# Two of K's three row blocks by seven block products instead of eight, with the sums on GpSimd

## The chip, the cores and the metric

The kernel runs on one core of one Trainium2 chip. The metric is the device time of one execution in microseconds (us); of several executions the median is taken.

## The reference

x is 64 batches of 32 rows by 512; ctx_4096 is 64 batches of 257 rows by 512. Six stages follow one another, each added to x. The change lies in the first, a cross attention in float32:

```
hidden = concat([context, latents])            # 257 + 32 = 289 rows per batch, 512 wide
q = latents @ Wq.T    -> 16 heads of 96        # latents = layernorm(x), 32 rows
k = hidden  @ Wk.T    ->  4 heads of 96        # 384 columns
v = hidden  @ Wv.T    ->  4 heads of 96
attn = softmax(q k^T / sqrt(96));  out = attn v @ Wo.T
```

After it come a self attention with rotary embedding, a linear layer with LoRA, a gated mix that uses a top-20 mask of ctx_4096 (the mask is computed during the first stage), a second self attention and a sparse linear layer.

## The kernel before

`phase_a` computes the cross attention for 16 tiles t of 128 rows, four batches j = 0 to 3 each; `phase_rest` does the other stages. Every engine's program is written out by hand as a list of stages, and semaphores join them: each engine runs its list strictly in order, so a stage that waits holds up everything behind it on its engine. `over_tiles` writes tile 0 and tile 15 out and loops over the others.

For one batch, TensorE (PE) forms K transposed (384 rows by 289 columns) as three row blocks of 128, each from four matmuls over the 512 contraction rows (`k_part`, L345), and V as two blocks (`v_part`, L352). K and V go through the two banks of `psKV` in turn: `next_bank` makes PE wait until the fill before last has been copied out. ScalarE (ACT) copies them out (`evac_k`, L505; `evac_v`, L513). `scores(t, j, h)` (L363) handles two of the four heads; VectorE (DVE) takes the row maxima (`row_max`, L637), ACT the exponentials (`exps`, L537), GpSimd (POOL) gathers the last 33 columns (`gather_tails`, L298), PE transposes the probabilities (`turn_probs`, L371 and L374), multiplies with V (`values`, L386 to L390), and turns a batch's output (`turn_out`, L411), which DVE copies to `OT` (`evac_ot`, L658). Once per tile PE runs the projection (`project`, L417) and the queries of the next tile (`q`, L335). DVE spends the rest of its time on the top-20 mask (`topk`, L678 and L682, eight steps per batch).

The K of batch j + 1 is made during batch j: row blocks 0 and 1 after `scores(t, j, 0)`, block 2 after `values(t, j, 0)`. The K of batch 0 is made at the head of the tile, where there are also the projection of the tile before and both V blocks. On ACT, the copy of block 2 stands behind `exps(t, j, 1)`. On DVE, batch j + 1 runs `evac_out`, `row_max(.., 0)`, top-k step 1, `evac_ot`, step 2, for j = 1 the row statistics of the next tile (`norm_stats`) and for j = 2 its normalisation (`norm`, L612), then `row_max(.., 1)` and steps 3 to 8. A float32 matmul shows as two passes in the trace, so one K block is 8 MATMUL rows.

```
def next_bank(t, n):
    wait(pe, kv_evac, kv(t, n) - 1)
    return psKV[:, kv_bank(t, n), :]
```

Of the kernel before, what the change touches and what calls it, by code (L numbers as in the profile page):

```python
# [10 lines left out]
ALU = mybir.AluOpType  # L11
# [20 lines left out]
GONE = -3.0e38  # L32

K_ROWS = [(0, 0, 96), (1, 64, 96), (1, 0, 64), (2, 0, 64), (3, 0, 96), (2, 64, 96)]
PARTS = [(0, 0, 0, 96, 0), (1, 0, 96, 128, 64), (1, 1, 0, 64, 0), (2, 1, 64, 128, 0), (3, 2, 0, 96, 0),
         (2, 2, 96, 128, 64)]
# [8 lines left out]
EARLY_LOADS, LATE_LOADS = 9, 11  # L47
# [10 lines left out]
def build_program(nc, a):  # L58
    ctx = ExitStack()
    with ctx:  # L60
# [19 lines left out]
        early_in = sem("early_in")  # L80
        n1 = norm_sems(sem, "n1")
# [6 lines left out]
        phase_a(nc, a, X, mask, ident, neghalf, x_tile, ps, early, early_in, n1, qkv_filled)  # L88
        phase_rest(nc, a, X, mask, ident, neghalf, x_tile, ps, early, early_in, n1, qkv_filled)


def phase_a(nc, a, X, mask, ident, neghalf, x_tile, ps, early, early_in, n1, qkv_filled):

    ctx = ExitStack()
    with ctx:
# [11 lines left out]
        hid = sb("hid", [P, TB, DC, S])  # L107
        xn = sb("xn", [P, D])
        xnT = sb("xnT", [P, DC, P])
        QT = sb("QT", [HD, KVH, TB, G * L])  # L110
        KT = sb("KT", [HD, 2, KVH, S])
        V = sb("V", [P, 2, 2, KW])
        Vlat = sb("Vlat", [P, KW])
# [52 lines left out]
        kv_evac = sem("kv_evac")  # L166
        s_filled = sem("s_filled")
# [18 lines left out]
        def kv(t, n):  # L186


            if isinstance(t, int) and t == 0 and n < 5:
                return 1 + n  # L190
            if isinstance(t, int) and t == -1 and n > 20:
                return 6 + n - 21
            return 4 + 24 * t + n
# [24 lines left out]
        def _(sp):  # L218
# [24 lines left out]
            def load_tail(t):  # L243
# [6 lines left out]
                wait(sp, kv_evac, kv(t - 1, 20) + 1)  # L250
# [8 lines left out]
            def body(t, first, last):  # L259
                if last:  # L260

                    for k, name in (("w_qkv", "w_qkv0"), ("w_o", "w_o0"), ("w_ffn", "w_ffn0"), ("loraA", "loraA"),
                                    ("cos", "cos"), ("sin", "sin"), ("causal", "causal"), ("block16", "block16"),
                                    ("jmask", "jmask")):
                        sp.dma_start(early[k][:], a[name]).then_inc(early_in, 16)
                    return
                for j in range(TB):
                    sp.wait_ge(kv_filled, kv(t, 5 * j + 4) + 1)
                    sp.wait_ge(topk_step, 8 * (TB * t + j) + 2)
                    sp.dma_start(hid[:, j, :, 0:CTX], a["ctxT"][TB * (t + 1) + j]).then_inc(ctx_in[j], 16)  # L270
# [5 lines left out]
        def _(pool):  # L276
# [4 lines left out]
            pool.wait_ge(zero_done, 4)  # L281

# [16 lines left out]

            def body(t, first, last):  # L300
                for j in range(TB):
                    for h in range(2):
                        if (j, h) == (1, 1):
                            next_rstd() if last else rstd_of(t + 1)
                        gather_tails(t, j, h)

            rstd_of(0)
            over_tiles(pool, body)

        @block.tensor  # L310
        def _(pe):
# [11 lines left out]
            def v_latents(t):  # L323
                out = next_bank(t - 1, 20)
# [5 lines left out]
            def q(t, k):  # L330
                out = next_bank(t - 1, 21 + k)
# [7 lines left out]
            def k_part(t, j, k):  # L339
                out = next_bank(t, 5 * j + k)  # L340
                if k == 0:
                    pe.wait_ge(ctx_in[j], 16 * (t + 1))
                    pe.wait_ge(m_evac, m_xt(t) + 1)
                for c in range(DC):
                    mm = pe.matmul(out[:, 0:S], WkT[:, c, P * k:P * k + P], hid[:, j, c, :],  # L345
                                   start=(c == 0), stop=(c == DC - 1))
                mm.then_inc(kv_filled, 1)

            def v_part(t, j, s):
                out = next_bank(t, 5 * j + 3 + s)  # L350
# [5 lines left out]
            def scores(t, j, h):  # L356
# [3 lines left out]
                if h == 0:  # L360
                    pe.wait_ge(kv_evac, kv(t, 5 * j + 2) + 1)
# [15 lines left out]
            def values(t, j, g):  # L377
                b = TB * t + j
                pe.wait_ge(pt_evac, 4 * b + g + 1)
                if g == 0:  # L380
                    pe.wait_ge(kv_evac, kv(t, 5 * j + 4) + 1)
# [17 lines left out]
            def next_qkv():  # L399
                pe.wait_ge(kv_evac, kv(NT - 1, 19) + 1)  # L400
# [30 lines left out]
            def body(t, first, last):  # L431
# [4 lines left out]
                k_part(t, 0, 2)  # L436
                v_part(t, 0, 0)
                v_part(t, 0, 1)
                if first:
# [3 lines left out]
                    pe.wait_ge(kv_evac, kv(-1, 23) + 1)  # L443
# [54 lines left out]
        def _(act):  # L498
            def evac_k(t, j, k):
                act.wait_ge(kv_filled, kv(t, 5 * j + k) + 1)  # L500
                if k == 0:
                    wait(act, s_filled, 2 * (TB * t + j) - 2)
                for g, tile, lo, hi, at in PARTS:
                    if tile == k:
                        ins = act.activation(KT[at:at + hi - lo, j % 2, g, :], psKV[lo:hi, kv_bank(t, 5 * j + k), 0:S],  # L505
                                             ACT.Copy)
                ins.then_inc(kv_evac, 1)

            def evac_v(t, j, s):
                act.wait_ge(kv_filled, kv(t, 5 * j + 3 + s) + 1)  # L510
                if s == 0:
                    wait(act, av_done, 4 * (TB * t + j) - 4)
                act.activation(V[:, j % 2, s, :], psKV[:, kv_bank(t, 5 * j + 3 + s), 0:KW], ACT.Copy).then_inc(kv_evac, 1)  # L513

            def evac_v_latents(t):
                wait(act, vtail_in, 16 * TAIL_LOADS * t)
                act.wait_ge(kv_filled, kv(t - 1, 20) + 1)
                act.activation(Vlat[:], psKV[:, kv_bank(t - 1, 20), 0:KW], ACT.Copy).then_inc(kv_evac, 1)

            def evac_q(t, k):  # L520
                wait(act, s_filled, 2 * TB * t)
                act.wait_ge(kv_filled, kv(t - 1, 21 + k) + 1)
# [1143 lines left out]
```

## Time and profile before

| what | before |
|---|---|
| three runs | 2140.99 us median (2138.29 to 2141.76) |
| profiled execution | 2136.47 us |
| its span, first to last instruction | 2134.4 us |
| granted TensorE clock, mean | 0.989 of full |
| PE, PEld (weight loads) busy | 96%, 69% of the span |
| DVE, ACT, POOL busy | 61%, 32%, 12% |
| K matmuls (L345) | 404.0 us busy, 1536 passes |
| POOL instructions | 360 |

The page gives busy time by engine, then groups of instructions by source line with their count, mean duration and the idle time of the engine ahead of them with the one that ended it. PE is busy nearly all the time up to about 1490 us, where `phase_a` ends. POOL's row of 40 slices reads 0 over that whole stretch. The timeline lists instructions in order of time; equal neighbours are merged, so the start of the next row less the start of a row is the pace at which the engine went through it, while the duration in the row also holds the drain of the last one.

### The profile page before, as it was taken

To read this page: it belongs to the slowest core of one execution; us is meant where nothing else is said; L and a number is where in the kernel's file an instruction comes from. 1 tells how busy PE (TensorE), PEld (TensorE's weight loads), DVE (VectorE), ACT (ScalarE), POOL (GpSimd) and SP (SyncE) were. 2 spreads that over 40 slices of the span, in tenths; PEclk is the share of its full clock that TensorE was granted. 3 is DMA by queue.
4 is the path that set the end of the run, shared out by engine and by line. 5 is a ranking of instruction groups with operands and counts; after the bars stand their busy time and mean duration, and the time that the engine had idled before them with its cause. 6 is when DMAs were issued, how large, how long until landed. Compare 5 with 4: busy or idle time off the path is not lost. (4 is left out here: it accounts for less than half of the span.)

```text
span 2134.4 us, 33623 instructions
## 1 busy us (share of the span) xinstructions
PE 2059.4 (96%) x10660; PEld 1480.4 (69%) x10660; DVE 1308.7 (61%) x4451; ACT 683.7 (32%) x1861; POOL 248.3 (12%) x360
## 2 busy tenths in 40 slices
PE   7999999999999999999999999999899999779998
PEld 5778677777767778677777867777566666466665
DVE  3736547484654747456483755747577777677885
ACT  2333333333332433333242433333223223122222
POOL 0000000000000000000000000000233333133332
PEclk9999999999999999999999999999999999889999
DMA  7101000010000101001010000120100000000000
GB/s 289 31 15 31 23 24 30 24 30 24 24 20 24 30 24 30 24 24 30 14 37 16 30 23 24 30 86 1 45 1 1 1 0 29 0 1 21 21 15 25
DMA packets 51991, 62.14 MB, mean 29 GB/s; under 512 B 14193, under 2 KB 47665, under 8 KB 51042
## 3 DMA queue, kind: packets, MB, share of 16 engines
q1 hardware_dynamic: 51938, 61.46, 9.1%
q8 instruction: 31, 0.51, 0.1%
q14 instruction: 22, 0.18, 0.0%
HBM read 54.00 MB, written 4.29 MB: 27 GB/s over the span
## 5 line engine op out<-in xcount | busy, mean ns | idle before, releaser
L345 PE MATMUL psLane<-hid,WkT 128*128 128x289 f32 x1536 | 404.0, 408 | 0.0
L352 PE MATMUL psLane<-WvT,hid 128*128 128x384 f32 x1024 | 348.7, 486 | 0.0
L345 PEld LDWEIGHTS psLane<-hid,WkT 128*128 128x128 f32 x1536 | 284.1, 190 | 72.7
L352 PEld LDWEIGHTS psLane<-WvT,hid 128*128 128x128 f32 x1024 | 189.8, 190 | 109.7
L537 ACT ACTIVATE probs<-psLane,nmax 128x289 f32<-128x289 f32 x256 | 126.2, 498 | 423.6 <-DVE nmax L640 423.6
L505 ACT ACTIVATE KT<-psLane 96x289 f32<-96x289 f32 (+2 forms) x384 | 155.8, 406 | 153.3 <-PE psLane L345 151.0
L298 POOL TENSOR_TENSOR tails<-probs,unit 128x66 f32<-128x66 f32 x128 | 38.1, 297 | 1387.3 <-ACT probs L537 1387.3
L678 DVE MAX8 top<-work 128x8 f32<-128x257 f32 x512 | 180.3, 414 | 2.7
L335 PE MATMUL psLane<-xnT,WqT 128*128 128x128 f32 x1536 | 176.6, 275 | 0.0
L335 PEld LDWEIGHTS psLane<-xnT,WqT 128*128 128x128 f32 x1536 | 174.8, 192 | 0.3
L663 DVE TENSOR_TENSOR X<-X,psLane 128x512 f32 (+1 forms) x16 | 11.0, 689 | 261.6 <-PE psLane L417 261.6
L417 PE MATMUL psLane<-WoT,OT 128*128 128x512 f32 x384 | 167.5, 592 | 1.4 <-DVE OT L658 1.4
L652 DVE TENSOR_TENSOR O<-psLane,rinv 128x384 f32<-128x384 f32 x64 | 35.7, 558 | 187.3 <-PE psLane L390 172.3
L363 PE MATMUL psLane<-KT,QT 96*128 96x289 f32 x512 | 146.1, 407 | 1.3 <-ACT QT L526 1.3
L513 ACT ACTIVATE V<-psLane 128x384 f32<-128x384 f32 x128 | 62.9, 491 | 243.2 <-PE psLane L352 243.2
L417 PEld LDWEIGHTS psLane<-WoT,OT 128*128 128x128 f32 x384 | 72.9, 190 | 89.8 <-issue 84.2
L637 DVE TENSOR_REDUCE rmax<-psLane 128x2 f32<-128x578 f32 x128 | 97.1, 758 | 58.7 <-PE psLane L363 57.5
L386 PEld LDWEIGHTS psLane<-V,probsT 128*128 128x128 f32 x512 | 87.3, 190 | 40.7 <-ACT probsT L544 8.5
L363 PEld LDWEIGHTS psLane<-KT,QT 96*128 96x128 f32 x512 | 90.8, 190 | 22.7 <-issue 7.2
L682 DVE MATCH_REPLACE8 work<-top,work 128x257 f32<-128x257 f32 x256 | 102.2, 411 | 0.0
L682 DVE MATCH_REPLACE8 work<-top,hid 128x257 f32<-128x257 f32 x256 | 102.2, 411 | 0.0
L682 DVE MATCH_REPLACE8 work<-top_last,work 128x257 f32<-128x257 f32 x256 | 102.2, 410 | 0.0
(190 smaller groups left out, 3138.2 us busy)
## 6 DMA issues: line engine op xcount, KB each, us to landing
hid<-in_ctxT SPq DMA_DIRECT2D x64, 514.0 KB, 3.8
y<-X SPq DMA_DIRECT2D x16, 256.0 KB, 2.0
X<-in_x SPq DMA_DIRECT2D x1, 3840.0 KB, 14.9
WqT<-in_WqT SPq DMA_DIRECT2D x4, 768.0 KB, 11.4
WoT<-in_WoT SPq DMA_DIRECT2D x1, 3072.0 KB, 21.7
Vtail<-Vlat SPq DMA_DIRECT2D x128, 24.0 KB
w_qkv<-in_w_qkv SPq DMA_DIRECT2D x2, 1536.0 KB, 6.5
w_ffn<-in_w_ffn SPq DMA_DIRECT2D x2, 1024.0 KB, 8.0
```

What stands on the lines that cost most here:

```text
L335: mm = pe.matmul(out[:, P * r:P * r + P], WqT[:, c, w:w + P], xnT[:, c, :], start=(c == 0), stop=(c == DC - 1))
L345: mm = pe.matmul(out[:, 0:S], WkT[:, c, P * k:P * k + P], hid[:, j, c, :], start=(c == 0), stop=(c == DC - 1))
L352: mm = pe.matmul(out[:, 0:KW], hid[:, j, c, P * s:P * s + P], WvT[:, c, :], start=(c == 0), stop=(c == DC - 1))
L363: mm = pe.matmul(psS[:, g % 2, 0:S], QT[:, g, j, :], KT[:, j % 2, g, :], start=True, stop=True)
L386: pe.matmul(out, probsT[:, g % 2, 0, :], V[:, j % 2, 0, cols], start=(g % 2 == 0), stop=False)
L417: mm = pe.matmul(psM, OT[:, n // G, n % G].rearrange("p j q -> p (j q)"), WoT[:, n, :], start=(n == 0), stop=(n == NKT * G - 1))
L505: ins = act.activation(KT[at:at + hi - lo, j % 2, g, :], psKV[lo:hi, kv_bank(t, 5 * j + k), 0:S], ACT.Copy)
L513: act.activation(V[:, j % 2, s, :], psKV[:, kv_bank(t, 5 * j + 3 + s), 0:KW], ACT.Copy).then_inc(kv_evac, 1)
L537: act.activation(probs[:, g, :], psS[:, g % 2, 0:S], ACT.Exp, bias=nmax[:, g:g + 1], scale=XSCALE, accum_out=rsum[:, j % 2, g:g + 1]).then ...
L637: dve.tensor_reduce(rmax[:, 2 * h:2 * h + 2], psS[:, :, 0:S], AX.X, ALU.max).then_inc(rmax_done, 1)
L678: ins = dve.max(top[step // 2][:, c, :], src[:, c, :] if step == 1 else work[:, c, :])
L682: ins = dve.match_replace(work[:, c, :], picked[:, c, :], src[:, c, :] if step == 2 else work[:, c, :], GONE)
```

## The change

Rows 0 to 255 of K (blocks m = 0, 1 of 128 rows), the contraction (k = 0, 1 of 256) and the 290 columns (s = 0, 1 of 145; one column of zeros is added) are cut in two each. The eight products of 2 by 2 block matrices are replaced by seven (Winograd's form of Strassen's scheme): four sums of weight blocks, made once (`combine_weights`), four sums of hidden blocks per batch (`sum_columns`), seven products, and seven sums of products (`add_products`). All sums run on POOL. The third row block is made as before. Per batch, PE now fills five banks for K: fill 0 is the third row block; fills 1, 2 and 3 hold products (1, 6), (7, 5) and (3, 4); fill 4 holds product 2. ACT copies fill 0 straight to `KT` in two instructions and each other fill to `kproducts` in one; POOL's last eight instructions per batch write the rest of `KT`, and `scores(t, j, 0)` waits for them. K's rows now stand in the order of the heads, so a head's 96 rows may lie at other partitions: `QT` and `KT` have 128 partitions, the foreign rows are set to zero once, and Q is copied out in seven pieces per tile, before six. The buffers of the sums lie in the space of `w_o` and `w_ffn` of the next stage, whose loads come later: SP waits for the last K before it issues them.

```
+KH = (S + 1) // 2
+K_FILLS = ((0,), (1, 6), (7, 5), (3, 4), (2,))
-EARLY_LOADS, LATE_LOADS = 9, 11
+EARLY_LOADS, LATE_LOADS = 7, 11
# SP, last tile
+                    sp.wait_ge(kv_filled, kv(NT - 1, 25) + 1)
+                    sp.wait_ge(k_ready, 8 * B)
+                    for k, name in (("w_o", "w_o0"), ("w_ffn", "w_ffn0")):
+                        sp.dma_start(early[k][:], a[name]).then_inc(square_in, 16)
# POOL
+            pool.memset(QT[:], 0.0).then_inc(rows_cleared, 1)
+            pool.memset(KT[:], 0.0).then_inc(rows_cleared, 1)
+            def sum_columns(t, j):
...
+                pool.wait_ge(ctx_in[j], 16 * (t + 1))
+                pool.wait_ge(m_evac, m_xt(t) + 1)
...
+                pool.tensor_tensor(ksums[:, 0], columns(0, 1), columns(0, 0), ALU.subtract).then_inc(ksum_step, 1)
+                pool.tensor_tensor(ksums[:, 2], columns(1, 1), columns(0, 1), ALU.subtract).then_inc(ksum_step, 1)
+                pool.wait_ge(ksum_step, 4 * b + 2)
+                pool.tensor_tensor(ksums[:, 1], columns(1, 1), ksums[:, 0], ALU.subtract).then_inc(ksum_step, 1)
+                pool.wait_ge(ksum_step, 4 * b + 3)
+                pool.tensor_tensor(ksums[:, 3], ksums[:, 1], columns(1, 0), ALU.subtract).then_inc(ksum_step, 1)
+            def k_block(t, j, m, s, x, y, op, done):
+                n = KH - s
+                for i, (g, tile, lo, hi) in enumerate(part for part in K_PARTS if part[1] == m):
+                    wait(pool, k_ready, 8 * (TB * t + j) + done + i)
+                    pool.tensor_tensor(KT[lo:hi, j % 2, g, KH * s:KH * s + n], x[lo:hi, 0:n], y[lo:hi, 0:n], op)\
+                        .then_inc(k_ready, 1)
+            def add_products(t, j):
+                b = TB * t + j
+                pool.wait_ge(kv_evac, kv(t, 7 * j + 1) + 1)
+                pool.tensor_tensor(u2, product(1), product(6), ALU.add).then_inc(kpost_step, 1)
+                pool.wait_ge(kv_evac, kv(t, 7 * j + 2) + 1)
+                pool.wait_ge(kpost_step, 3 * b + 1)
+                pool.tensor_tensor(u3, u2, product(7), ALU.add).then_inc(kpost_step, 1)
+                pool.wait_ge(kpost_step, 3 * b + 2)
+                pool.tensor_tensor(u4, u2, product(5), ALU.add).then_inc(kpost_step, 1)
+                pool.wait_ge(kpost_step, 3 * b + 3)
...
+                k_block(t, j, 1, 1, u3, product(5), ALU.add, 0)
+                pool.wait_ge(kv_evac, kv(t, 7 * j + 3) + 1)
+                k_block(t, j, 0, 1, u4, product(3), ALU.add, 2)
+                k_block(t, j, 1, 0, u3, product(4), ALU.subtract, 4)
+                pool.wait_ge(kv_evac, kv(t, 7 * j + 4) + 1)
+                k_block(t, j, 0, 0, product(1), product(2), ALU.add, 6)
+                pool.wait_ge(k_ready, 8 * b + 8)
             def body(t, first, last):
+                add_products(t, 0)
+                sum_columns(t, 1)
                 for j in range(TB):
+                    gather_tails(t, j, 0)
+                    if j == TB - 1 and not last:
+                        sum_columns(t + 1, 0)
+                    if j == 1:
+                        next_rstd() if last else rstd_of(t + 1)
+                    gather_tails(t, j, 1)
+                    if j < TB - 1:
+                        add_products(t, j + 1)
+                    if j < TB - 2:
+                        sum_columns(t, j + 2)
# PE
+                    for i, n in enumerate(K_FILLS[f]):
+                        if n == 6:
+                            pe.wait_ge(ksum_step, 4 * (TB * t + j) + 4)
...
+                        mm = k_product(out[:, KH * i:KH * i + KH], j, n)
                 if h == 0:
+                    pe.wait_ge(k_ready, 8 * b + 8)
                     if j < TB - 1:
                         k_part(t, j + 1, 0)
+                        k_part(t, j + 1, 1)
                         if j:
                             turn_out(t, j - 1)
-                        k_part(t, j + 1, 1)
...
                     if j < TB - 1:
                         k_part(t, j + 1, 2)
+                        k_part(t, j + 1, 3)
                         values(t, j, 1)
+                        k_part(t, j + 1, 4)
# ACT, behind exps(t, j, 1)
                         evac_k(t, j + 1, 2)
+                        evac_k(t, j + 1, 3)
+                        evac_k(t, j + 1, 4)
```

In the lists of instructions below, L-numbers are those of each kernel's own source, one row is one matmul (two passes of the trace) or one instruction of POOL, and the brackets name the semaphores waited for. `w_o` and `w_ffn` stand for the buffers of the sums: `w_o` holds the sums of hidden, `w_ffn` those of the weights and the products.

The program of tile 0 is shown. PE in batch j = 1, from the first K block behind `scores(t, 1, 0)` on, before:

```order
L345 MATMUL psLane<-hid,WkT 128x289 [waits m_evac,ctx_in2,kv_evac]
L345 MATMUL psLane<-hid,WkT 128x289 x3
L411 MATMUL psLane<-ident,O 128x128 [waits o_evac,m_evac]
L411 MATMUL psLane<-ident,O 128x128 x2
L345 MATMUL psLane<-hid,WkT 128x289 [waits kv_evac]
L345 MATMUL psLane<-hid,WkT 128x289 x3
L371 MATMUL psLane<-ident,probs 128x128 [waits pt_evac,exp_done]
L371 MATMUL psLane<-ident,probs 128x128
L371 MATMUL psLane<-ident,probs 128x128 [waits pt_evac,exp_done]
L371 MATMUL psLane<-ident,probs 128x128
L374 MATMUL psLane<-ident,tails 66x128 [waits tails_ready]
L363 MATMUL psLane<-KT,QT 128x289 [waits exp_done]
```

and now, from fill 1 on:

```order
L437 MATMUL psLane<-hid,WkT 128x145 [waits kv_evac]
L437 MATMUL psLane<-hid,WkT 128x145
L437 MATMUL psLane<-w_o,w_ffn 128x145 [waits ksum_step]
L437 MATMUL psLane<-w_o,w_ffn 128x145
L520 MATMUL psLane<-ident,O 128x128 [waits o_evac,m_evac]
L520 MATMUL psLane<-ident,O 128x128 x2
L480 MATMUL psLane<-ident,probs 128x128 [waits pt_evac,exp_done]
L480 MATMUL psLane<-ident,probs 128x128
L480 MATMUL psLane<-ident,probs 128x128 [waits pt_evac,exp_done]
L480 MATMUL psLane<-ident,probs 128x128
L483 MATMUL psLane<-ident,tails 66x128 [waits tails_ready]
L472 MATMUL psLane<-KT,QT 128x289 [waits exp_done]
```

The transposes of the output, L411 before and L520 now, stood between the two K blocks and now stand behind fill 1, whose second product waits for POOL's sums.

PE in the same batch from `values` on, before:

```order
L386 MATMUL psLane<-V,probsT 128x96 [waits vtail_in,o_evac,kv_evac,pt_evac]
L387 MATMUL psLane<-V,probsT 128x96
L345 MATMUL psLane<-hid,WkT 128x289 [waits kv_evac]
L345 MATMUL psLane<-hid,WkT 128x289 x3
L386 MATMUL psLane<-V,probsT 128x96 [waits pt_evac]
L387 MATMUL psLane<-V,probsT 128x96
L390 MATMUL psLane<-Vtail,probsTail 128x192
L352 MATMUL psLane<-WvT,hid 128x384 [waits kv_evac]
L352 MATMUL psLane<-WvT,hid 128x384 x3
```

and now:

```order
L437 MATMUL psLane<-w_o,w_ffn 128x145 [waits kv_evac]
L437 MATMUL psLane<-w_o,w_ffn 128x145 x3
L437 MATMUL psLane<-hid,w_ffn 128x145 [waits kv_evac]
L437 MATMUL psLane<-hid,w_ffn 128x145
L437 MATMUL psLane<-w_o,WkT 128x145 x2
L495 MATMUL psLane<-V,probsT 128x96 [waits pt_evac]
L496 MATMUL psLane<-V,probsT 128x96
L499 MATMUL psLane<-Vtail,probsTail 128x192
L437 MATMUL psLane<-hid,WkT 128x145 [waits kv_evac]
L437 MATMUL psLane<-hid,WkT 128x145
L460 MATMUL psLane<-WvT,hid 128x384 [waits kv_evac]
L460 MATMUL psLane<-WvT,hid 128x384 x3
```

Before, a V block stood behind `values(.., 1)`, and it took the bank of K's row block 1. Now fill 4 stands there (the last but one pair of rows), and takes the bank of fill 2, which was filled only just before.

POOL in tile 0, from its start to the end of its tails, before:

```order
L286 TENSOR_TENSOR rstd<-veps,neghalf 128x1 [waits veps_ready,zero_done]
L298 TENSOR_TENSOR tails<-probs,unit 128x66 [waits exp_done] x2
L298 TENSOR_TENSOR tails<-probs,unit 128x66 [waits pt_filled,exp_done]
L286 TENSOR_TENSOR rstd<-veps,neghalf 128x1 [waits veps_ready,xn_ready]
L298 TENSOR_TENSOR tails<-probs,unit 128x66 [waits pt_filled,exp_done] x5
```

and now, from the row statistics within batch 1 to the start of batch 2:

```order
L304 TENSOR_TENSOR rstd<-veps,neghalf 128x1 [waits veps_ready,xn_ready]
L316 TENSOR_TENSOR tails<-probs,unit 128x66 [waits pt_filled,exp_done]
L362 TENSOR_TENSOR w_ffn<-w_ffn 128x145 [waits kv_evac]
L365 TENSOR_TENSOR w_ffn<-w_ffn 128x145 [waits kpost_step,kv_evac]
L367 TENSOR_TENSOR w_ffn<-w_ffn 128x145 [waits kpost_step]
L355 TENSOR_TENSOR KT<-w_ffn 64x144 [waits k_ready,s_filled,kpost_step]
L355 TENSOR_TENSOR KT<-w_ffn 64x144 [waits k_ready]
L355 TENSOR_TENSOR KT<-w_ffn 128x144 [waits k_ready,kv_evac]
L355 TENSOR_TENSOR KT<-w_ffn 32x144 [waits k_ready]
L355 TENSOR_TENSOR KT<-w_ffn 64x145 [waits k_ready] x2
L355 TENSOR_TENSOR KT<-w_ffn 128x145 [waits k_ready,kv_evac]
L355 TENSOR_TENSOR KT<-w_ffn 32x145 [waits k_ready]
```

Behind the second gather of batch 1 there now stand the eleven instructions of `add_products(t, 2)`, each of which waits for the one before it.

## Rows read from the trace of the kernel before

**Rows 1.** The page, part 1: busy us (share of the span) x instructions.

```profile
PE 2059.4 (96%) x10660; PEld 1480.4 (69%) x10660; DVE 1308.7 (61%) x4451; ACT 683.7 (32%) x1861; POOL 248.3 (12%) x360
```

**Rows 2.** Waits of PE up to 1500 us: total us, times, longest.

```profile
PE psLane L386 <- DMA Vtail<-Vlat: 1.9, 1, 1.9
```

**Rows 3.** Groups: line, shape, count, busy us, mean ns, idle before; copies of K.

```profile
L505 ACT ACTIVATE KT<-psLane 96x289 f32<-96x289 f32 x128 | 51.8, 405 | 80.1 <-PE psLane L345 80.1
```

**Rows 4.** Timeline of PE, one tile: start us, us, engine, line, operation.

```profile
599.75 1.14 PE L363 MATMUL psLane<-KT,QT 96*128 96x289 f32 x4
...
657.91 3.74 PE L335 MATMUL psLane<-xnT,WqT 128*128 128x128 f32 x32
...
692.05 1.14 PE L363 MATMUL psLane<-KT,QT 96*128 96x289 f32 x4
```

**Rows 5.** Timeline of PE, batches 1 and 2 of that tile.

```profile
616.48 1.14 PE L363 MATMUL psLane<-KT,QT 96*128 96x289 f32 x4
617.46 2.12 PE L345 MATMUL psLane<-hid,WkT 128*128 128x289 f32 x8
619.42 0.49 PE L411 MATMUL psLane<-ident,O 128*128 128x128 f32 x3
...
621.70 0.60 PE L371 MATMUL psLane<-ident,probs 128*128 128x128 f32 x4
...
622.24 1.14 PE L363 MATMUL psLane<-KT,QT 96*128 96x289 f32 x4
...
623.71 2.14 PE L345 MATMUL psLane<-hid,WkT 128*128 128x289 f32 x8
...
626.46 2.75 PE L352 MATMUL psLane<-WvT,hid 128*128 128x384 f32 x8
...
633.39 1.14 PE L363 MATMUL psLane<-KT,QT 96*128 96x289 f32 x4
...
647.71 1.14 PE L363 MATMUL psLane<-KT,QT 96*128 96x289 f32 x4
```

**Rows 6.** Timeline of DVE, batch 1, and the normalisation in batch 2.

```profile
617.66 0.76 DVE L637 TENSOR_REDUCE rmax<-psLane 128x2 f32<-128x578 f32 x1 [0.36 <-PE psLane L363]
...
620.10 0.54 DVE L658 COPY OT<-psLane 128x384 f32<-128x384 f32 x1
...
622.15 0.68 DVE L601 BATCH_NORM_STATS2 stats<-X 128x6 f32 x1
...
623.42 0.76 DVE L637 TENSOR_REDUCE rmax<-psLane 128x2 f32<-128x578 f32 x1 [0.18 <-PE psLane L363]
...
639.05 0.54 DVE L612 TENSOR_SCALAR xn<-X,mv,rstd 128x512 f32 x1
```

**Rows 7.** Timeline of ACT and of POOL, batch 1: exponentials and tails.

```profile
624.42 0.50 ACT L537 ACTIVATE probs<-psLane,nmax 128x289 f32<-128x289 f32 x1 [0.86 <-DVE nmax L640]
...
625.57 0.30 POOL L298 TENSOR_TENSOR tails<-probs,unit 128x66 f32<-128x66 f32 x1 [1.71 <-ACT probs L537]
```

**Rows 8.** Groups of POOL: 66, 640, 512 columns, and the power of one.

```profile
L298 POOL TENSOR_TENSOR tails<-probs,unit 128x66 f32<-128x66 f32 x128 | 38.1, 297 | 1387.3 <-ACT probs L537 1387.3
...
L981 POOL TENSOR_TENSOR lanes<-lanes 128x640 f32<-128x640 f32 x16 | 24.6, 1539 | 53.7 <-DVE lanes L1151 53.7
L992 POOL TENSOR_TENSOR lanes<-posT,lanes 128x512 f32<-128x512 f32 x16 | 20.3, 1270 | 22.1 <-DVE lanes L1206 22.1
...
L286 POOL TENSOR_TENSOR rstd<-veps,neghalf 128x1 f32<-128x1 f32 x16 | 8.8, 549 | 46.8 <-DVE veps L607 46.8
```

**Rows 9.** Timelines of POOL and DVE in a later stage.

```profile
1804.88 0.78 POOL L813 TENSOR_TENSOR lane_rstd<-lane_veps,neghalf 128x1 f32<-128x1 f32 x1 [1.18 <-DVE lane_veps L808]
...
1804.72 0.54 DVE L818 TENSOR_SCALAR lane_xn<-X,lane_mv,lane_rstd 128x512 f32 x1
```

**Rows 10.** Windows: length, busy us of PE, PEld, DVE, ACT, POOL; granted clock, DMA.

```profile
51.00:55.00 4.00, 4.00 (x14) 2.94 (x13) 3.83 (x21) 0.10 (x1) 0.19 (x1) 0.57 0.39 127
1494.00:1497.00 3.00, 0.91 (x4) 0.60 (x5) 3.00 (x14) 0.00 (x0) 0.00 (x0) 1.00 0.00 0
```

More of the change, by code:

```diff
@@ L260, in body @@
                 if last:
-                    for k, name in (("w_qkv", "w_qkv0"), ("w_o", "w_o0"), ("w_ffn", "w_ffn0"), ("loraA", "loraA"),
+                    for k, name in (("w_qkv", "w_qkv0"), ("loraA", "loraA"),
                                     ("cos", "cos"), ("sin", "sin"), ("causal", "causal"), ("block16", "block16"),
@@ new lines, in _ @@
+            at_product = {n: 2 * (f - 1) + i for f, fill in enumerate(K_FILLS) for i, n in enumerate(fill)}
+            product = lambda n: kproducts[:, at_product[n], :]
+            u2, u3, u4 = product(6), product(7), product(6)
+            def k_block(t, j, m, s, x, y, op, done):
[4 more added lines that the diff above has]
+                        .then_inc(k_ready, 1)
@@ L307, in _ @@
             rstd_of(0)
+            combine_weights()
+            sum_columns(0, 0)
             over_tiles(pool, body)
@@ L435, in body @@
                     turn_out(t - 1, TB - 1)
-                k_part(t, 0, 2)
+                for f in range(2, 5):
+                    k_part(t, 0, f)
                 v_part(t, 0, 0)
@@ L498, in _, with evac_k @@
         def _(act):
-            def evac_k(t, j, k):
-                act.wait_ge(kv_filled, kv(t, 5 * j + k) + 1)
-                if k == 0:
+            def evac_k(t, j, f):
+                act.wait_ge(kv_filled, kv(t, 7 * j + f) + 1)
+                bank = psKV[:, kv_bank(t, 7 * j + f)]
+                if f == 0:
                     wait(act, s_filled, 2 * (TB * t + j) - 2)
[L503 to L506, printed above, removed]
+                    if isinstance(t, int) and t == 0:
+                        act.wait_ge(rows_cleared, 2)
+                    for g, tile, lo, hi in K_PARTS:
+                        if tile == 2:
+                            ins = act.activation(KT[lo:hi, j % 2, g, :], bank[lo:hi, 0:S], ACT.Copy)
+                else:
+                    if f == 1:
+                        wait(act, k_ready, 8 * (TB * t + j))
+                    at, n = 2 * (f - 1), len(K_FILLS[f])
+                    ins = act.activation(kproducts[:, at:at + n].rearrange("p a n -> p (a n)"), bank[:, 0:KH * n], ACT.Copy)
@@ L523, in evac_q @@
-                src = psKV[:, kv_bank(t - 1, 21 + k), :].rearrange("p (r j q) -> p r j q", r=G, j=TB)
-                for g, tile, lo, hi, at in PARTS:
+                act.wait_ge(kv_filled, kv(t - 1, 29 + k) + 1)
+                src = psKV[:, kv_bank(t - 1, 29 + k), :].rearrange("p (r j q) -> p r j q", r=G, j=TB)
+                if isinstance(t, int) and t == 0:
+                    act.wait_ge(rows_cleared, 2)
+                for g, tile, lo, hi in Q_PARTS:
                     if tile == k:
-                        ins = act.activation(QT[at:at + hi - lo, g].rearrange("p j (r q) -> p r j q", r=G), src[lo:hi],
-                                             ACT.Copy)
+                        ins = act.activation(QT[lo:hi, g].rearrange("p j (r q) -> p r j q", r=G), src[lo:hi], ACT.Copy)
@@ L553, in body @@
             def body(t, first, last):
-                for k in range(NKT):
-                    evac_k(t, 0, k)
+                for f in range(5):
+                    evac_k(t, 0, f)
                 evac_v(t, 0, 0)
@@ L1580, in k_perm @@
 def k_perm():
[L1581 removed]
+    return np.arange(KW)
 def by_chunks(w):
```

123 lines of the change are left out of this document (81 added, 42 removed).

## The prediction

> **What bounds the kernel now.** I read the page first: PE is busy for 96% of the span, the next engine for 61% [rows 1]. Then the list of PE's waits: once the first loads have landed, the longest up to 1500 us is 1.9 us, and it comes once [rows 2]. So in the first stage PE is the only bound, and every other engine has time left. The timeline gives the pace: one tile of four batches takes 692.05 - 599.75 = 92.3 us, sixteen tiles some 1477 us [rows 4]. What PE loses or gains per tile is lost or gained sixteen times. The question is therefore what the change takes from PE's list, and which of its new waits come later than the work that should cover them.
>
> **What PE's work shrinks by.** Eight passes of 289 columns take 619.42 - 617.46 = 1.96 us, 0.245 each [rows 5]. For 32 passes of 128 columns 3.74 us, less the 0.275 of the last, over 31 steps, give 0.112 [rows 4]. The line through both has 0.00083 us a column, and 145 columns come to 0.126. Sixteen passes of 289 (3.92 us) become 28 of 145 (3.53): 0.39 us less per batch, 1.6 per tile, 25 in all. A fill of two products takes 1.01 us, fill 4 0.50.
>
> **What is put on POOL.** Its two-operand instructions take 1.27 us for 512 columns and 1.54 for 640, 0.0021 a column, and 0.297 for 66 [rows 8]. From above that makes 0.50 us for 145 columns, from below 0.46; I take 0.49. Each of the eleven instructions of `add_products` waits for the one before. What such a step costs on POOL no row shows; ends are 0.03 us (as DVE follows itself) and 0.20 (PE to DVE: scores end at 623.22, `row_max` starts at 623.42 [rows 6]); I take 0.09. The chain then is 11 x 0.58 = 6.4 us, with ends 5.4 and 7.7. `sum_columns` is four of 290 columns at 0.80 and two such steps, 3.4 us. With 9.8 us of new work in 23, POOL has room on average. The order decides.
>
> **Walk through batch 1** (us from its first scores, 616.48 in [rows 5]). PE: scores to 0.98, fill 0 to 2.94, fill 1 to 3.95, the transposes of the output 0.32 (619.42 to 621.70 less one K block) to 4.27; before, they ended at 3.26. DVE needs them for `evac_ot`, which started at 3.62 (620.10) right behind top-k step 1 [rows 6]. Now it starts at 4.47, and behind it stand the copy (0.54), step 2 (1.51) and the statistics (to 623.24, 1.09): DVE is free at 7.61, before at 6.76. PE has long finished the second scores (4.81 to 5.79). So `row_max(1)` starts at 7.63. From its start to the exponentials 1.00 us pass (623.42 to 624.42), both take 0.97 [rows 6, 7], and only then does ACT copy fill 2, 0.41 [rows 3]. For the way from there to PE's next pass I take 0.25; 0.10 and 0.35 are its ends. Fill 4 can start at 10.26. PE is there earlier: 5.79, values 0.49, fills 2 and 3 2.02, values 0.77 (623.71 to 626.46, less the block's 1.98), 9.07. Before, the same place asked only for row block 1, long copied. **A stall of 1.19 us.** Behind it fill 4 takes 0.50, and V, transposes and values 6.93 (626.46 to 633.39): the batch lasts 17.69 us where it lasted 16.91: +0.78.
>
> POOL in this batch: the tails follow the exponentials' start by 1.15 us and take 0.30 [rows 7]; the chain starts at 10.08 and ends at 16.5, under cover. POOL's sums for batch 3 then end at 19.9, that is 2.2 us into batch 2, where product 6 wants them at 3.4: covered by 1.2 us.
>
> **Batch 2.** `evac_ot` is late in the same way; behind step 2 stands the normalisation, 0.54 [rows 6], `row_max(1)` starts at 7.10, fill 4 may start at 9.73, PE waits 0.66. POOL's tails end at 9.55, its chain at 15.95, and the first scores of batch 3 start at 16.20. PE alone would be there at 9.73 + 0.50 + 4.34 (V, transposes, values; there is one V block less here) = 14.57, and before took 647.71 - 633.39 = 14.32. **A second stall, 1.63 us; the batch +1.88.** This one is set by POOL alone.
>
> **The other parts of a tile.** Batch 0 has no output to transpose: `row_max(1)` at 5.7, fill 2 copied at 8.05, fill 4 wanted at 8.7; POOL ready at 14.5 of 16.3: -0.39. At the head fill 3 is copied 0.86 us after its end (hand-over 0.20, copy 0.41, 0.25) and fill 4 covers 0.50 of it, so V waits 0.36: -0.03; the chain there lies beside V and the projection, ten us of cover. Batch 3 makes no K: 0. There POOL's sums for the next tile hold its second gather to about 10.4, wanted at 14. If that cover went, the transposes would wait for it.
>
> **Sum.** -0.39 + 0.78 + 1.88 + 0 - 0.03 = +2.24 us per tile, +36 for sixteen. Once, at the start: three copies of the last Q part in place of two, 0.6 us, ahead of the first scores; the clearing of `QT` and `KT` and the weights' sums are hidden by PE's wait for the first loads. The later loads of `w_o` and `w_ffn` cost nothing: between the issue, at the last batch's scores, and their use lie that batch and a projection, some 30 us (647.71 to 692.05 less the next tile's Q, K and V [rows 4, 5]); without that cover the next stage would wait for the transfer. ACT's copies: six instructions per batch before and after, 0. All this against the profiled execution, 2136.47: 2173. The median of the runs shown is 4.5 us higher, so I forecast **2177 us**.
>
> **A rule against the change.** In a later stage one POOL instruction beside a DVE TENSOR_SCALAR of 0.54 us took 0.78 us [rows 9], where its like take 0.549 [rows 8]. The Trainium skill, "SBUF — State Buffer", section "Who interferes with whom", says that such DVE operations and any POOL operation lock one port pair, so that the second waits the first out; the trace agrees in direction. By that rule the mask's last DVE operation and a small copy, 0.4 us together in POOL's chain, would make the sum 6 us more in batch 2's stall. I leave them out of the sum and keep them in the range, as the tails, which ran beside MAX8, all took 0.30.
>
> **Rivals.**
> (a) Only the waits behind the exponentials bind, because POOL's instructions run faster than their durations (at 0.44 us a step). For it: POOL's durations are rough. Against: each step waits for the end of the last. Batch 2 then gains 0.25 instead of 1.88, the tile 0.6, the whole 10: 2151. Chance 0.06.
> (b) The cover holds at both places: faster. Mechanism: fill 2 is copied before PE asks for fill 4, as it would be if `row_max(1)` did not stand behind the late `evac_ot`, and POOL's chain fits into 4.7 us. Place: fill 4 and the first scores of batch 3. It decides when the stalls of a tile, 3.8 us in my walk, come below 1.6. Price: -25, 2116. Against it is that 1.19 us would have to be wrong in a chain of rows. Chance 0.09.
> (c) The stalls cost the clock too. PE's idle of 1.9 us [rows 2], just ahead of the first window of rows 10, was followed there by a mean granted clock of 0.57 over 4 us (it fell to half), while 0.91 us of work in 3 kept it at 1.00 [rows 10]. A stall of 1.6 lies between. Price 4 x 0.43 = 1.7 us per tile, 27: 2204. Chance 0.09.
> (d) MATCH_REPLACE on DVE also holds POOL up; no row of before shows the two together for long. Eight of them, mean delay 0.2, lengthen the chain by 1.6 us, +1.9 us per tile in batches 1 and 2: 2207. Chance 0.06.
>
> **How the numbers follow.** The forecast has 0.70. Its own range comes from the chain: with 5.4 us batch 2 loses 1.1, +20 in all, and with shorter hand-overs +12; with 7.7 us batches 1 and 2 lose 1.1 and 3.2, +62. That is 2153 to 2203. To leave out no more than 2 in 10 I widen it to 2150 and 2208, which takes in (a), (c) and (d). A measurement here tells 0.2%, 4.3 us, from no change. Faster by more: (b) and a little, 0.10; within: 0.04; slower: 0.86.
>
> **What would show it.** Right: K's narrow passes at a pace of 0.126 us; `evac_ot` in batches 1 and 2 at 4.5 us; a gap of PE before fill 4 in batches 1 and 2 put down to ACT's copy, and one of 1.6 us before the scores of batch 3 put down to POOL; tiles of 94.5 us; POOL busy about 30% in this stage. Wrong: no gap at either place, POOL steps far from 0.58 us, PE waiting for the sums before product 6, or a clock below 1 within the tiles.

## The result, and the profile after

| | before | after |
|---|---|---|
| runs | 2138.29 us median of 5 (2133.64 to 2141.76) | 2153.66 us median of 5 (2151.71 to 2156.09) |
| profiled execution, its span | 2136.47, 2134.4 us | 2152.95, 2150.9 us |
| granted TensorE clock, mean | 0.989 | 0.990 |

The ratio is 1.0077 (95% interval 1.0058 to 1.0097): the change makes the kernel 0.8% slower, 15 us, where 36 were forecast. The direction held, the size did not.

The page of the changed kernel, part 1: busy us (share of the span) x instructions, beside [rows 1].

```profile
PE 2041.6 (95%) x11428; PEld 1517.2 (71%) x11428; DVE 1316.6 (61%) x4451; ACT 666.2 (31%) x1877; POOL 776.8 (36%) x1327
```

PE has 17.8 us less to do, and the span is 16.5 us longer. So some 34 us of new idle time must exist. The waits of PE up to 1500 us show nearly all of it in two rows (total us, times, longest), 33.4 together. Neither row was there before: the list then had only waits that came once, all at the start or the end of the stage, the longest 8.9 for the first loads and then the 1.9 of [rows 2].

```profile
PE psLane L437 <- ACT w_ffn L625: 18.8, 32, 1.1
PE psLane L472 <- POOL KT L355: 14.6, 16, 1.0
```

L437 is the matmul of the products, and the wait is that of fill 4. L472 is the scores, and the wait is that of a batch's first ones. 32 is two batches in each of sixteen tiles, 16 is one: the two places of the forecast. The timeline of PE over one tile, to be laid beside [rows 4, 5]; the four batches start at 606.10, 622.16, 639.73 and 655.12, the next tile at 699.39.

```profile
606.10 1.14 PE L472 MATMUL psLane<-KT,QT 128*128 128x289 f32 x4
...
622.16 1.14 PE L472 MATMUL psLane<-KT,QT 128*128 128x289 f32 x4
623.14 2.11 PE L446 MATMUL psLane<-hid,WkT 128*128 128x289 f32 x8
...
632.21 0.76 PE L437 MATMUL psLane<-hid,WkT 128*128 128x145 f32 x4 [0.92 <-ACT w_ffn L625]
...
639.73 1.14 PE L472 MATMUL psLane<-KT,QT 128*128 128x289 f32 x4
...
649.12 0.76 PE L437 MATMUL psLane<-hid,WkT 128*128 128x145 f32 x4 [0.26 <-ACT w_ffn L625]
...
655.12 1.24 PE L472 MATMUL psLane<-KT,QT 128*128 128x289 f32 x4 [0.90 <-POOL KT L355]
```

```profile
699.39 0.90 PE L472 MATMUL psLane<-KT,QT 128*128 128x289 f32 x3
```

The differences of these starts (batch 3 and the head of the next tile in one column, since the next tile's start closes both):

| us | batch 0 | batch 1 | batch 2 | batch 3 and head | tile |
|---|---|---|---|---|---|
| before | 16.73 | 16.91 | 14.32 | 44.34 | 92.30 |
| forecast | 16.34 | 17.69 | 16.20 | 44.31 | 94.54 |
| after | 16.06 | 17.57 | 15.39 | 44.27 | 93.29 |

The tile is 0.99 us longer, and sixteen make 15.8 of the 16.5 of the span. The first scores of all come at 42.29 us, where it was 42.03; that is 0.3 later, not the 0.6 of the forecast. The chain that makes batch 1 wait stands in the timeline of DVE, and after it ACT's:

```profile
626.60 0.56 DVE L782 COPY OT<-psLane 128x384 f32<-128x384 f32 x1 [0.75 <-PE psLane L520]
...
628.67 0.68 DVE L725 BATCH_NORM_STATS2 stats<-X 128x6 f32 x1
...
629.78 0.76 DVE L761 TENSOR_REDUCE rmax<-psLane 128x2 f32<-128x578 f32 x1
```

```profile
630.78 0.50 ACT L657 ACTIVATE probs<-psLane,nmax 128x289 f32<-128x289 f32 x1 [3.06 <-DVE nmax L764]
...
631.75 0.71 ACT L625 ACTIVATE w_ffn<-psLane 128x290 f32<-128x290 f32 x2
```

DVE sits idle for 0.75 us until PE has turned the output; the copy starts 4.44 us after the batch's first scores (it was 3.62 [rows 6]), `row_max(1)` at 7.62, the exponentials at 8.62, the copies of fills 2 and 3 at 9.59, and fill 4 at 10.05. Batch 2's other wait is POOL's, from the second tails to the last piece of `KT`:

```profile
648.84 0.30 POOL L316 TENSOR_TENSOR tails<-probs,unit 128x66 f32<-128x66 f32 x1 [5.18 <-ACT probs L657]
649.10 0.44 POOL L362 TENSOR_TENSOR w_ffn<-w_ffn 128x145 f32<-128x145 f32 x1
649.62 0.45 POOL L365 TENSOR_TENSOR w_ffn<-w_ffn 128x145 f32<-128x145 f32 x1
650.14 0.44 POOL L367 TENSOR_TENSOR w_ffn<-w_ffn 128x145 f32<-128x145 f32 x1
650.83 4.24 POOL L355 TENSOR_TENSOR KT<-w_ffn 64x144 f32<-64x144 f32 x8 [0.24 <-POOL w_ffn L367]
```

From 649.10 to 655.07 this is one chain of eleven steps, and PE starts its scores 0.05 us after its end.

### The profile page after: what moved, and what is told of

The parts are those of the page before. It is cut to its first block and busy times, and to the rows that moved or that the text cites. A ratio compares the mean times of both kernels' runs of the same rounds, so it can differ in the third digit from the quotient of the medians.

```text
span 2150.9 us, 37658 instructions
## 1 busy us (share of the span) xinstructions
PE 2041.6 (95%) x11428; PEld 1517.2 (71%) x11428; DVE 1316.6 (61%) x4451; ACT 666.2 (31%) x1877; POOL 776.8 (36%) x1327
## 5 line engine op out<-in xcount | busy, mean ns | idle before, releaser
L355 POOL TENSOR_TENSOR KT<-w_ffn 64x144 f32<-64x144 f32 (+5 forms) x512 | 236.7, 462 | 50.5 <-POOL w_ffn L367 13.7
L472 PE MATMUL psLane<-KT,QT 128*128 128x289 f32 x512 | 147.6, 410 | 16.5 <-POOL KT L355 14.6
L446 PE MATMUL psLane<-hid,WkT 128*128 128x289 f32 x512 | 135.2, 406 | 0.0
L937 POOL TENSOR_TENSOR lane_rstd<-lane_veps,neghalf 128x1 f32<-128x1 f32 x79 | 52.9, 669 | 198.1 <-DVE lane_veps L932 198.1
L472 PEld LDWEIGHTS psLane<-KT,QT 128*128 128x128 f32 x512 | 90.2, 191 | 42.3 <-POOL KT L355 16.7
L437 PE MATMUL psLane<-w_o,w_ffn 128*128 128x145 f32 x768 | 117.6, 289 | 0.0
L625 ACT ACTIVATE w_ffn<-psLane 128x290 f32<-128x290 f32 (+1 forms) x256 | 94.2, 383 | 71.4 <-PE psLane L437 63.5
L446 PEld LDWEIGHTS psLane<-hid,WkT 128*128 128x128 f32 x512 | 96.6, 189 | 26.4
L362 POOL TENSOR_TENSOR w_ffn<-w_ffn 128x145 f32<-128x145 f32 x64 | 28.0, 438 | 238.9 <-ACT w_ffn L625 238.9
```

The costliest lines, as they stand in the source:

```text
L355: pool.tensor_tensor(KT[lo:hi, j % 2, g, KH * s:KH * s + n], x[lo:hi, 0:n], y[lo:hi, 0:n], op)\
L437: mm = pe.matmul(out, left(c), right(c), start=(c == 0), stop=(c == 1))
L446: mm = pe.matmul(out[:, 0:S], WkT[:, c, 2 * P:3 * P], hid[:, j, c, 0:S], start=(c == 0), stop=(c == DC - 1))
L472: mm = pe.matmul(psS[:, g % 2, 0:S], QT[:, g, j, :], KT[:, j % 2, g, :], start=True, stop=True)
L625: ins = act.activation(kproducts[:, at:at + n].rearrange("p a n -> p (a n)"), bank[:, 0:KH * n], ACT.Copy)
```

## The experiments

The theory is that two chains decide, each at its place: (1) the output's transposes behind fill 1 make DVE late, and so the exponentials, and so ACT's copy of fill 2, for which fill 4 waits; (2) POOL's eleven steps behind the second tails hold the first scores of batch 3. The rivals: the copies themselves, or PE's changed order as such, or the clock. Times are medians, with the ratio to the kernel before and its 95% interval. Differences "to the change" below are of the spans of the profiled executions, and a batch's time is from first scores to first scores, read in one tile in the middle.

The spans also hold something that doesn't follow the edits. In batch 0 of the first tile the clock fell to its lower level in the kernel before, the change, e3, e8 and e9, and that batch took 19.0 to 20.5 us. In e1, e4, e5 and e6 it didn't fall there, and the batch took 17.8 to 18.3. So a span can be off by some 2 us, and the batches' times are the surer reading.

**The transposes back between fill 0 and fill 1 (e1).**

```
                         k_part(t, j + 1, 0)
-                        k_part(t, j + 1, 1)
                         if j:
                             turn_out(t, j - 1)
+                        k_part(t, j + 1, 1)
```

> The changed kernel, with the transposes of the output put back between the two K fills (fill 0, transposes, fill 1), as they stood before. Theory (two late waits, fill 4 behind ACT's copy of fill 2, and the first scores of batch 3 behind POOL's chain, both set by when row_max of the second pair starts): DVE's evac_ot starts 0.9 us earlier in batches 1 and 2, row_max(1) at 6.8 and 6.2 us after the batch's first scores (now 7.6 and 7.0); the stall before fill 4 shrinks from 1.1 to 0.3 in batch 1 and goes in batch 2, the wait for POOL shrinks from 1.1 to about 0.9 at an end 0.8 us earlier. Tile 93.3 -> 91.6 us, execution 27 us shorter than the changed kernel, 10 us shorter than before. Rival (POOL's chain sets the pace wherever it ends, the order of the transposes is covered): within 4 us of the changed kernel. Rival (fill 4 alone): 13 us shorter, batch 2 unchanged.

Measured: 2124.57 us, 0.9944 of before (0.993 to 0.9957); the span is 30.2 us below the change's. PE's wait for ACT's copy is all but gone: in batch 1 fill 4 starts 0.23 us after PE gets there, where it was 1.09 in the change, and in batch 2 it doesn't wait. POOL's fell from 14.6 to 8.9:

```profile
PE psLane L472 <- POOL KT L355: 8.9, 16, 0.6
```

Batch 1 takes 16.72 us (17.57), batch 2 14.53 (15.39). `row_max(1)` is back at 6.77 us after the batch's first scores:

```profile
616.64 0.76 DVE L761 TENSOR_REDUCE rmax<-psLane 128x2 f32<-128x578 f32 x1
```

One move of three transposes by 1 us turns +0.8% into -0.6%. Sixteen tiles of 1.72 us less make 27.5, as was expected. The move also takes 0.3 us from POOL's wait in batch 2, since POOL's chain hangs on the same exponentials.

**The same move in the kernel before (e9)**, whose list has the transposes between its two K blocks:

```
                         k_part(t, j + 1, 0)
+                        k_part(t, j + 1, 1)
                         if j:
                             turn_out(t, j - 1)
-                        k_part(t, j + 1, 1)
```

> The kernel before with one line moved: the transposes of the output behind the second K block instead of between the two. evac_ot and row_max(1) then come about 0.9 us (batch 1) and 0.2 to 0.9 us (batch 2) later, as in the changed kernel. Theory (lateness costs only where the work between the second scores and the first wait on the exponentials is too short; here it is 5.8 us instead of 3.1): 0, within 3 us of the kernel before. Rival (the later row_max costs by itself): 0.8 us in batches 1 and 2, 25 us longer.

Measured: 2140.40 us, 1.0017 of before (1.0007 to 1.0027), 4 us by the medians where at most 3 were expected; span +2.7 us. Batches 1 and 2 read 16.83 and 14.42 us, as before within 0.1. The rest, 0.24, is in batch 3, where PE's order is untouched. The timelines of PE show it in the transposes of the first pair's probabilities, before and with the line moved:

```profile
651.60 0.60 PE L371 MATMUL psLane<-ident,probs 128*128 128x128 f32 x4
```

```profile
652.24 0.83 PE L371 MATMUL psLane<-ident,probs 128*128 128x128 f32 x4
```

DVE's list is still late there (its `row_max(0)` of batch 3 starts 1.93 us after the batch's first scores, where it was 1.18), and so are the exponentials, 3.15 for 2.41. So lateness does cost a little by itself, at the place with the least cover. The order of PE alone costs 0.3 us a tile where no fill waits for the copy of row block 2, and 1.7 (93.29 less e1's 91.57) where fill 4 does. The rival "PE's order as such" is out: it is the pair, a late `evac_ot` and a new consumer of the copy behind it.

**Fill 2 copied before the second exponentials (e3).**

```
+                    if j < TB - 1:
+                        evac_k(t, j + 1, 2)
                     exps(t, j, 1)
...
-                        evac_k(t, j + 1, 2)
```

> The changed kernel, with ACT's copy of fill 2 ahead of the second pair's exponentials instead of behind them. Theory: fill 4 no longer waits in batches 1 and 2; in batch 1 the V block behind it then waits 0.6 us for the copy of fill 3, so 0.5 of 1.1 us is won; in batch 2 the same time is lost again before the first scores of batch 3, since POOL's chain starts when it did. Batch 0's exponentials start 0.8 us later, under cover. Tile -0.5 us, execution 9 us shorter than the changed kernel. Rival (both stalls add up independently, the POOL one a fixed 1 us): tile -0.9, 14 us shorter.

Measured: 2146.59 us, 1.005 of before (1.0037 to 1.0064); span 7.9 us below the change's. Batch 1 gains 0.49 (17.08), batch 2 nothing (15.38): fill 4 no longer waits, and POOL's wait takes up what it leaves. In the list of waits (the second row is V behind fill 4, which now waits for the copy of fill 3):

```profile
PE psLane L472 <- POOL KT L355: 22.9, 16, 1.6
...
PE psLane L460 <- ACT w_ffn L625: 6.7, 16, 0.6
```

The expected 9 us came out as 7.9. In batch 2 the two waits lie one behind the other on PE, but they are not added: POOL's chain ends when it ends, and what PE no longer waits ahead of fill 4 it waits at the end. So the walk had it: the batch's length was "set by POOL alone".

**Two more steps in POOL's chain (e4)**, which write to a place that nobody reads.

```
+            idle = spare[1][:, 1200:1200 + KH]
...
+                for i in range(3, 5):
+                    pool.wait_ge(kpost_step, 5 * b + i)
+                    pool.tensor_tensor(idle, product(1), product(5), ALU.add).then_inc(kpost_step, 1)
```

> The changed kernel, with two more instructions of 145 columns in POOL's chain of every batch (their result is not used). Theory: each step costs 0.52 us; batches 0, 1 and the tile's head have 2.0, 1.6 and several us of cover and show nothing; batch 2 shows all of it, +1.04 us per tile, execution 17 us longer than the changed kernel. Rival (POOL's work slows the others through shared ports, in all batches): +1 us or more in every batch, 50 us and more. Rival (POOL's chain is not what PE waits for): within 4 us.

Measured: 2189.37 us, 1.0245 of before (1.0231 to 1.0259); span 32.5 us above the change's, about twice what the steps take. Thirteen steps take 7.08 us where eleven took 5.97, 0.56 for each of the two. Batches 0 and 1 stand still (16.05, 17.57), so that POOL's work as such slows nobody, and batch 2 grows by 1.11, 18 us in all. The other half is in batch 3 and the head, 45.95 us where the change has 44.27. The waits and the windows of one tile's end show why (length, busy us of PE, PEld, DVE, ACT, POOL; granted clock, DMA):

```profile
PE psLane L476 <- POOL KT L356: 32.5, 16, 2.1
```

```profile
665.00:666.00 1.00, 0.00 (x0) 0.00 (x0) 0.65 (x3) 0.00 (x0) 0.92 (x2) 1.00 0.00 0
666.00:667.00 1.00, 0.43 (x2) 0.38 (x3) 0.00 (x0) 0.00 (x0) 0.44 (x2) 1.00 0.00 0
667.00:668.00 1.00, 1.00 (x4) 0.73 (x3) 0.00 (x0) 0.00 (x0) 0.00 (x0) 0.54 0.00 0
668.00:669.00 1.00, 1.00 (x3) 0.55 (x3) 0.57 (x1) 0.00 (x0) 0.00 (x0) 0.50 0.00 0
669.00:670.00 1.00, 1.00 (x3) 0.51 (x2) 0.82 (x5) 0.34 (x1) 0.00 (x0) 0.50 0.00 0
670.00:671.00 1.00, 1.00 (x4) 0.58 (x3) 0.95 (x3) 0.74 (x4) 0.05 (x1) 0.75 0.00 0
```

PE idles for 2.0 us until 666.57, and then the clock falls from its upper level, 2.4 GHz, to 1.2 GHz for some 3.4 us. That is rival (c)'s mechanism, at an idle time that the change itself doesn't reach. It doesn't strike every time, though. The sixteen waits are all 2.01 to 2.14 us, and a stretch of 3.5 us that begins 0.6 us behind the scores' start ran at 1.00 in six tiles and at 0.51 to 0.65 in ten (PE only: length, busy us; clock, DMA):

```profile
190.34:193.84 3.50, 3.50 (x16) 1.00 0.00 0
284.73:288.23 3.50, 3.50 (x8) 0.51 0.00 0
```

Ten times 1.68 us (45.95 less 44.27) and sixteen times 1.1 make 34 us, against 32.5 of span (the rest is mostly the first tile, where batch 0 took 2.0 us less than in the change). In the kernel with fill 2 copied first, whose waits are 1.4 us and in the first and the last tile 1.57, one of sixteen fell (the first, 0.54 over the same stretch). In the change, with 0.9 and at most 1.05, none did.

**u2, the first sum of products, ahead of the second gather (e5)**, so that the first of the eleven steps is done early.

```
+            def add_first(t, j):
+                pool.wait_ge(kv_evac, kv(t, 7 * j + 1) + 1)
+                pool.tensor_tensor(u2, product(1), product(6), ALU.add).then_inc(kpost_step, 1)
...
                     gather_tails(t, j, 0)
...
+                    if j < TB - 1:
+                        add_first(t, j + 1)
                     gather_tails(t, j, 1)
```

> The changed kernel, with the first of POOL's eleven sums (product 1 + product 6, ready long before) put ahead of the gather of the second pair's tails. Theory: the chain behind the exponentials has ten steps, batch 2 ends 0.52 us earlier, the others stay; tile -0.5, execution 8 us shorter than the changed kernel. Rival (POOL's busy time, not the place of its steps, counts): 0, within 3 us.

Measured: 2149.11 us, 1.006 of before (1.0046 to 1.0074); span 5.3 us below the change's. Batch 2 gains 0.37 (15.02), less than a step of 0.52: in the change u2 starts 0.26 us after the tails' start, and here the next step starts 0.39 after it. Batch 1 loses 0.08, and the timelines of DVE and POOL show where:

```profile
627.36 0.25 DVE L770 TENSOR_SCALAR nmax<-rmax 128x2 f32<-128x2 f32 x1
```

```profile
627.15 0.44 POOL L361 TENSOR_TENSOR w_ffn<-w_ffn 128x145 f32<-128x145 f32 x1
```

`nmax` takes 0.25 us where it takes 0.17 in the change, and ends with the POOL instruction beside it. It stands in the chain to the exponentials, so PE's wait for fill 4 grows from 18.8 to 20.4 us.

**A copy of ACT more in the first half of the batch (e8)**, to see whether batch 0's gain beyond the passes comes from ACT's shorter list.

```
                     if f == 1:
                         wait(act, k_ready, 8 * (TB * t + j))
+                        act.activation(spare[1][:, 1200:1200 + S], bank[:, 0:S], ACT.Copy)
```

> The changed kernel with one more ACT copy of 289 columns ahead of the copy of fill 1 in every batch (its result is not used). It tests why batch 0 gained 0.67 us where narrower passes explain 0.44. Theory (before, ACT's four copies of K between the exponentials and the probabilities' copies made values(0) wait 0.15 us and start cold by 0.07 in each batch; now there are three): batch 0 loses 0.15 to 0.25 us again, the others 0 to 0.07; execution 3 to 5 us longer than the changed kernel. Rival (the passes themselves save more than I read): 0.

Measured: 2154.72 us, 1.0085 of before (1.0064 to 1.0105), span 0.9 us below the change's: a miss. Only batch 0 moved, by 0.06 us: its first `values` row is 0.42 long, not 0.36, a matmul whose weights came late. No wait for ACT appeared. The copy did not delay `probsT` (the copies of the transposed probabilities) enough. They start 0.93 us ahead of PE's arrival at `values` in the change, 0.65 here and 0.48 before, and beyond the passes batch 0 loses 0, 0.06 and 0.23. That order agrees with the idea, but no run gave the whole loss back.

**All that helped, together (e6)**: the transposes between fills 0 and 1, fill 2 copied first in batch 1 only (in the others its copy would delay exponentials that POOL waits for), u2 early, and with it the wait for the scores that last read this `KT`.

```
-                        k_part(t, j + 1, 1)
                         if j:
                             turn_out(t, j - 1)
+                        k_part(t, j + 1, 1)
...
+                    if j == 1:
+                        evac_k(t, j + 1, 2)
                     exps(t, j, 1)
...
+            def add_first(t, j):
...
+                wait(pool, s_filled, 2 * (TB * t + j) - 2)
```

> The changed kernel with three moves together: the transposes back between fills 0 and 1; in batch 1 ACT's copy of fill 2 ahead of the exponentials; POOL's first sum (and its wait for the scores of two batches ago) ahead of the gather of the second pair's tails. Theory: no stall before fill 4; batch 1 takes 16.4 us (17.6 in the changed kernel, 16.9 before), batch 2 14.1 to 14.2 (15.5, 14.3), with a wait for POOL of 0.3 to 0.4 left. Tile 90.9, execution about 39 us shorter than the changed kernel and 22 shorter than the kernel before. Rival (the time that narrow passes save is given back at the next wait wherever one is removed): no better than the kernel before.

Measured: 2115.49 us (median of 4), 0.9897 of before (0.9874 to 0.992); span 39.5 us below the change's, 23.0 below that of before. The tile is 90.79 us, 1.51 less than before, near the four times 0.39 that the prediction had for the passes alone (by the passes as measured, four times 0.44). The nearness is partly luck. The parts are 0.67 in batch 0, 0.52 in batch 1, 0.24 in batch 2 and 0.07 in the rest: batch 0 has a gain that nobody forecast, and batch 2 still waits 0.1 for POOL. Batch 2 takes 14.08:

```profile
622.16 1.14 PE L478 MATMUL psLane<-KT,QT 128*128 128x289 f32 x4
...
636.24 1.24 PE L478 MATMUL psLane<-KT,QT 128*128 128x289 f32 x4
```

This beats both kernels. The scheme was sound; its place in the lists was not.

## Why the prediction was right in direction and wrong in size

By its own steps, each per tile:

- **The two stalls: right in place and cause.** `evac_ot` at 4.47 forecast, 4.44 measured; `row_max(1)` in batch 1 at 7.63, measured 7.62; fill 4 at 10.26, measured 10.05. From PE's arrival to the start, fill 4 waits 1.09 us in batch 1 and 0.43 in batch 2 (1.19 and 0.66 forecast), and the scores of batch 3 wait 1.06 (1.63 forecast). The single move of e1 took nearly all of the first away, and e4 and e5 moved the second by what they added to POOL's chain or took from it.
- **The step that failed is the price of POOL's chain**, "11 x 0.58 = 6.4 us", and with it batch 2's "+1.88", measured +1.07. From 649.10 to 655.07 the chain takes 5.97. Seven of its eleven instructions were 0.44 long and four 0.49, where I took 0.49 for all. The gap behind each is 0.08 (I took 0.09), but for one of 0.24 before the eight. So the steps are 0.51 to 0.57 apart, and the chain is 0.43 shorter than forecast, some 0.35 of it by the durations. The 0.43 are more than half of batch 2's error of 0.81.
- **Hand-over to PE, taken as 0.25**: 0.05, from POOL as from ACT. 0.20 of batch 2's error.
- **The chain's start at 9.55**: 9.37 measured, because `row_max(1)` in batch 2 began at 6.97, not 7.10, and u2 starts 0.26 us after the tails' start, in their last 0.04. 0.18, the rest of batch 2.
- **Batch 1**: 17.69 forecast, 17.57 measured, fill 4's start 0.21 earlier (the shorter hand-over) against 0.09 lost in its row, 0.76 for 0.66: the first matmul behind a wait is some 0.1 longer.
- **Batch 0: -0.39 forecast, -0.67 measured.** The 28 passes of 145 columns took 3.50 us where sixteen of 289 took 3.94, 0.05 more of a gain than I had. Beyond that, before, PE's scores ended at 606.16 and `values(t, 0, 0)` began at 606.31, in a row 0.43 long for 0.36, while ACT was still copying `probsT`, late behind its four copies of K:

```profile
606.31 0.43 PE L386 MATMUL psLane<-V,probsT 128*128 128x96 f32 x2
```

```profile
604.83 0.82 ACT L505 ACTIVATE KT<-psLane 64x289 f32<-64x289 f32 x2 [0.87 <-PE psLane L345]
605.68 0.66 ACT L544 ACTIVATE probsT<-psLane 128x256 f32<-128x256 f32 x2
```

  After, there is no wait. I had not looked for a wait that the change removes, only for those it adds. The list of waits leaves it out, since it is too small.
- **Head and batch 3**: -0.03 forecast for the two together, -0.07 measured. The head gained 0.16, with the wait behind fill 4 there (0.16 instead of 0.36), and batch 3 lost 0.09 in its first scores behind the wait for POOL.
- **Sum**: 2.24 forecast, 0.99 measured. The errors have one sign: -0.28, -0.12, -0.81, -0.04. Sixteen times 1.25 make 20 of the 23 us by which 2177 was too high; most of the rest is the 4.5 added for the median, where run and median now lie 0.7 apart. Two smaller slips of the prediction change nothing in the forecast. For a chain of 5.4 us batch 2 would lose 0.9, not 1.1, and the "+20 in all" has it so. And "POOL busy about 30%" does not follow from the durations used, which make 39% of a tile (44 x 0.49, 16 x 0.80 and 8 x 0.30 us in 94.5); measured are 38% (35.1 of 93.3 us).
- **The rule on the port.** DVE's mask, a TENSOR_SCALAR of 128 columns, took 226 to 228 ns in all 64 instances before, and after it has this row (duration ns min/median/max):

```profile
L813 DVE TENSOR_SCALAR mask<-work x64: 226/383/409, 55.4 to 1516.6; 128x128 f32 x56, 128x128 uint8<-128x128 f32 x8
```

  POOL's own steps stay at 0.44 beside it. So POOL is not held up, DVE is, and nothing waits for the mask there. In all 43 instances over 0.3 us the mask begins beside a POOL instruction that was there first, and ends 0.08 us behind its end. The Trainium skill, "SBUF — State Buffer", section "Who interferes with whom", has it that who comes second waits for the whole instruction; the trace agrees, here and for `nmax` in e5. Leaving the rule out of the sum was right, but my reason was not the one. POOL's chain has gaps of mostly 0.08 us, so that DVE will nearly always find it there first; that is my reading, and no run separates it.
- **The rivals.** (a) was partly true: a step costs 0.54 on average, neither 0.58 nor 0.44, and the wait for POOL stayed. (b) did not happen in the change, but in e6: with the cover given back the kernel lies at 2115, where its price was 2116, partly by luck, as said there. (c): the clock was 1.00 behind all sixteen waits; e4 has the mechanism at 2.0 us. (d): MATCH_REPLACE and POOL's steps ran side by side at their usual 0.41 and 0.44.

What stays open: batch 0's 0.23 us beyond the passes, which no run took apart; why seven of POOL's instructions were 0.44 long and four 0.49; and what POOL's chain would be without a wait between each two of its eight last instructions, which was not tried.

## What to carry to other kernels

When a change gives an old copy a new reader, look for what else in the same edit makes the copy late: here the moved transposes alone cost 0.2%, the seven products alone gained 0.6%, and the two together lost 0.8%. A chain of n small dependent steps is the term to price most carefully, because its error is multiplied by n and by the tiles. Here a duration read off rows of 66 and 512 columns was 0.05 us too long in seven of eleven steps, and even the lower of its two ends, 0.46, lay above the 0.44 that they took. And a list in order is worth a pass for slack before an idea is given up: the same arithmetic gave +0.8% as written and -1.0% with three stages moved.

## What the runs showed of the hardware

- Equal waits of PE did not have equal consequences. Behind 2.01 to 2.14 us of idle time the granted clock fell to its lower level in ten tiles of sixteen, behind 1.4 to 1.6 in one of sixteen, behind 0.9 to 1.05 in none. A fall costs 1.7 us here, more than the added 1.1 us of waiting.
- A POOL TENSOR_TENSOR of 144 or 145 columns takes 0.44 to 0.49 us on 32, 64 or 128 partitions alike, and a dependent one starts mostly 0.08 us behind its end, 0.51 to 0.57 after its start.
- A DVE TENSOR_SCALAR beside such an instruction goes from 0.23 to 0.38 to 0.40 us (128 columns) and from 0.17 to 0.25 (2 columns), and ends 0.02 to 0.08 us behind it, while POOL's own time stays.
- Float32 passes of 145 columns run at 0.125 us, those of 289 at 0.244, with their weight loads hidden: at this size splitting a matmul in two costs PE 0.006 us.
